# The turned probabilities of an attention kernel: another store queue, other places for weight work, and a last batch that is turned on TensorE

## The reference

```python
qh = (q_in @ wq + bq).reshape(b, q_len, H, K)
kh = (kv_in @ wk + bk).reshape(b, t, H, K)
vh = (kv_in @ wv + bv).reshape(b, t, H, K)
kh = jnp.concatenate([kh, jnp.broadcast_to(bias_k, (b, 1, H, K))], axis=1)
vh = jnp.concatenate([vh, jnp.broadcast_to(bias_v, (b, 1, H, K))], axis=1)
logits = jnp.einsum('bqhk,bthk->bhqt', qh, kh) / scale
weights = jax.nn.softmax(logits, axis=-1)
ctx = jnp.einsum('bhqt,bthk->bqhk', weights, vh).reshape(b, q_len, H * K)
return ctx @ wo + bo
```

## Time and profile before

| | us | share of the span |
|---|---|---|
| median of three runs | 2407.84 | |
| the profiled execution | 2412.1 | |
| its span, 36258 instructions | 2409.9 | |
| PE busy (matmuls) | 2258.8 | 94% |
| PE weight loads (beside the matmuls) | 2027.3 | 84% |
| DVE busy | 1384.3 | 57% |
| ACT busy | 1116.7 | 46% |
| POOL busy | 609.1 | 25% |

### The profile page before, as it was taken

The page is one execution under the profiler, slowest core; times in us unless marked ns, Lnnn a source line. Parts: engine busy times, 40 slices in busy tenths (PEclk is TensorE's granted clock), DMA queues, the critical chain, the costliest instruction groups (busy, mean ns, idle before and its releaser), DMA issues.

```text
span 2409.9 us, 36258 instructions
## 1 busy us (share of the span) xinstructions
PE 2258.8 (94%) x12323; PEld 2027.3 (84%) x12323; DVE 1384.3 (57%) x3102; ACT 1116.7 (46%) x2276; POOL 609.1 (25%) x919
## 2 busy tenths in 40 slices
PE   7999999997999999999988998999998998988999
PEld 6777788897998888898887897988888898977888
DVE  6877863515665665665653525665665565553843
ACT  5777742533444444444433543444444444443421
POOL 2111074401222222222222301222222223122421
PEclk9999999999999999999999999999999999999999
DMA  6322156646877877877864647787887887765110
GB/s 200 120 86 99 62 162 194 211 158 217 276 262 226 274 258 227 273 261 226 277 201 127 211 162 221 255 271 240 259 266 241 263 271 237 236 189 160 57 53 31
DMA packets 326902, 483.18 MB, mean 200 GB/s; under 512 B 65726, under 2 KB 250962, under 8 KB 324674
## 3 DMA queue, kind: packets, MB, share of 16 engines
q1 hardware_dynamic: 326722, 480.87, 61.9%
HBM read 370.30 MB, written 110.49 MB: 200 GB/s over the span
## 4 chain that ended last, share of the span: by engine, by line
PE 67%; DVE 10%; POOL 6%; ACT 6%; issue 6%; DMA 4%; SPq 1%; DVEq 0%; ACTq 0%; POOLq 0%
PE ps_o L1820 7%; PE ps_o L1822 6%; PE ps_o L1821 6%; PE ps_v L1820 5%; PE ps_v L1822 5%; PE ps_v L1821 5%; POOL pt_lo L912 5%; PE ps_k L1820 5%; PE ps_k L1821 4%; PE ps_k L1822 4%; PE ps_s L1820 3%; PE ps_s L1822 3%; PE ps_s L1821 3%; DMA turned_probabilities<-blocks 3%; PE ps_t L1821 2%
## 5 line engine op out<-in xcount | busy, mean ns | idle before, releaser
L1207 ACT ACTIVATE prob<-ps_s,row_columns 128x376 f32<-128x376 f32 x256 | 147.1, 575 | 378.0 <-DVE row_columns L1600 377.9
L912 POOL TENSOR_TENSOR pt_lo<-pt_lo,pt_hi 128x512 fp32r<-128x512 f32 x192 | 245.3, 1307 | 227.2 <-ACT pt_hi L1183 227.2
L904 POOL CAST k_hi<-xk_hi 128x1 fp32r<-128x1 f32 x256 | 52.8, 206 | 895.5 <-PE ps_s L1822 895.5
L1820 PE MATMUL ps_v<-pt_hi,ckd 128*128 128x448 f32 (+1 forms) x384 | 155.1, 404 | 81.4 <-POOL pt_lo L912 63.0
L1820 PE MATMUL ps_k<-cs_hi,w_a_hi 128*128 128x376 f32 x636 | 219.5, 345 | 0.0
L1821 PE MATMUL ps_k<-cs_lo,w_a_hi 128*128 128x376 f32 x636 | 214.7, 338 | 0.0
L1822 PE MATMUL ps_k<-cs_hi,w_a_lo 128*128 128x376 f32 x636 | 213.2, 335 | 0.0
L859 POOL TENSOR_TENSOR w_b_lo<-w_raw_b,w_b_hi 128x512 fp32r<-128x512 f32 x80 | 109.3, 1391 | 349.4 <-ACT w_b_hi L963 349.3
L1616 DVE STREAM_TRANSPOSE blocks<-prob 128x384 f32<-128x384 f32 x256 | 148.1, 579 | 68.4 <-DMA turned_probabilities<-blocks 60.3
L1488 DVE TENSOR_SCALAR prob<-prob,row_columns 128x375 f32<-128x375 f32 (+1 forms) x384 | 177.4, 462 | 4.5
L1485 DVE RECIPROCAL row_columns<-row_columns 128x1 f32<-128x1 f32 (+1 forms) x384 | 62.5, 163 | 196.1 <-ACT prob L1207 188.5
(11 more groups left out here) (290 smaller groups left out, 6391.8 us busy)
## 6 DMA issues: line engine op xcount, KB each, us to landing
ckd<-context_by_key_halves SPq DMA_DIRECT2D x256, 384.0 KB, 5.1
turned_probabilities<-blocks SPq DMA_DIRECT2D x64, 768.0 KB, 3.8
pt_lo<-turned_probabilities SPq DMA_DIRECT2D x256, 192.0 KB, 4.0
cs_hi<-context_halves SPq DMA_DIRECT2D x64, 752.0 KB, 5.8
cs_lo<-context_halves SPq DMA_DIRECT2D x64, 752.0 KB, 7.4
w_raw_b<-in_blocks_b SPq DMA_DIRECT2D x104, 256.0 KB, 3.5
w_raw_a<-in_blocks_a SPq DMA_DIRECT2D x104, 256.0 KB, 4.1
q<-q_scratch SPq DMA_DIRECT2D x64, 256.0 KB, 3.6
```

The source lines that it names most:

```text
L912: pool.tensor_tensor(lo, lo.bitcast(F32), hi, ALU.subtract).then_inc(t_lo, 1)
L1207: act.activation(prob[buf][:, 0:KW], ps_s[buf][:, 0:KW], ACT.Exp, bias=max_neg[:, buf:buf + 1], accum_out=prob_sum[:, buf:buf + 1]).then_i ...
L1820: pe.matmul(out, w_h, m_h, start=first, stop=False)
```

## The change

- **Store.** `store_blocks` goes from SP's queue to ACT's: at t = 2, behind `key_hi` and `sum_hi`, ahead of the exponential. SP keeps the loads.
- **Halves of the turned weights.** `turned_hi` goes ahead of the exponential of t = 0. POOL subtracts by key tile (three instructions of four runs of 128 columns), and `context_sum(0)` waits for one key tile at a time.
- **Weight work.** The split of block b goes from t = 0 and 1 of b2 to t = 2 and 3; the loads go from b2 to b3: block a at t = 0, block b at t = 1 (`fetches`).
- **Queries.** SP's part of the late query pieces goes to the end of its slot.
- **Banks.** Head outputs use ps_o[0] and ps_t[1] in turn and wait for the eviction of the one before the last; the outputs at the end are whole.
- **Last batch of an attend** (`place.final`). Its probabilities aren't stored: PE transposes them (24 transpositions in both attends) into banks, ACT and DVE read halves from there. b6's sum ends in the slots t = 2 and 3; the epilogue has b7's sum, then the head outputs, and rows 0 and 1 of `project` follow them.

Three places show how instructions move; names in these rows are of buffers, and the first word is the line.

The diff, cut to its core:

```diff
+        self.fetches = isinstance(self.b, int) and self.b == 3 and att.layer and group > 0
-        return {0: (0, 1), 1: (2, 3)}.get(t, ()) if self.att.layer and self.loads else ()
+        return {2: (0, 1), 3: (2, 3)}.get(t, ()) if self.att.layer and self.loads else ()
...
+            if place.final and t >= 2:
+                return {2: ((last, 0), (last, 1), (last, 2)), 3: ((last, 3),)}[t]
...
+        def last_bank(t):
+
+            return (ps_t[1], ps_k, ps_t[0], ps_t[1])[t]
...
-            return (ps_o[0], ps_s[0], ps_s[1], ps_t[1])[t] if place.final else ps_o[0]
+            return (ps_o[0], ps_t[1])[t % 2]
...
-                        if query_piece(place, t):
-                            last_query(query, a, skip, query_piece(place, t))
                         if t == 1 and place.after(2):
                             load_q(place.after(2))
                         if t == 2:
                             store_extra(place)
-                            store_blocks(place)
                         if t == 3:
-                            load_turned(place)
+                            if not place.final:
+                                load_turned(place)
                             if place.quarter == 3:
                                 load_extra(place)
                         for head in heads(place, t):
                             store_head(quad_before(place), head)
                         for summed, d in chunks(place, t):
                             load_by_key(summed.next(), d)
-                        if t == 1 and place.loads:
+                        if query_piece(place, t):
+                            last_query(query, a, skip, query_piece(place, t))
+                        if t == 0 and place.fetches:
+                            load_block(0, place.block_a + 1)
+                        if t == 1 and place.fetches:
                             load_block(1, place.block_b + 1)
-                            load_block(0, place.block_a + 1)
...
                 def turned_lo(place):
-                    pool.wait_ge(t_hi, place.visit + 1)
-                    for i in range(3):
-                        part = slice(i * D, (i + 1) * D)
-                        hi, lo = (pt[place.parity][s][:, part] for s in range(2))
+                    pool.wait_ge(t_hi, turned_batches(place) + 1)
+                    for j in range(3):
+                        hi, lo = (key_tile(s, place, j) for s in range(2))
                         pool.tensor_tensor(lo, lo.bitcast(F32), hi, ALU.subtract).then_inc(t_lo, 1)
...
+                def store_blocks(place):
+                    act.wait_ge(block_turn, turned_heads(place, NT))
+                    act.dma_start(turned_scr[place.parity], blocks[:]).then_inc(blocks_out, 16)
+
+                def last_turned_hi(place, t):
+                    act.wait_ge(last_turn, NT * a + t + 1)
+                    if t == 0:
+                        act.wait_ge(c_mm, NT * place.visit - NT)
+                    act.activation(last_place(0, place, t), last_turned(t), ACT.Identity).then_inc(last_hi, 1)
...
-                    wait(act, block_turn, unit_1(place, t) - 1)
+                    if place.final and t >= 2:
+                        act.wait_ge(last_turn, NT * a + t - 1)
+                    elif place.head and place.parity == 0 and t < 2:
+                        wait(act, last_turn, NT * a)
+                    else:
+                        wait(act, block_turn, turned_heads(place, t) - 1)
...
                         for summed, d in chunks(place, t):
                             sum_hi(summed, d)
+                            if place.final and t == 2 and d < 2:
+                                last_turned_hi(place, d + 2)
+                        if t == 0 and place.before():
+                            turned_hi(place.before())
+                        if place.final and t < 2:
+                            last_turned_hi(place, t)
+                        if t == 2 and not place.final:
+                            store_blocks(place)
                         if place.key(t + 2):
                             exp(*place.key(t + 2))
-                        if t == 0 and place.before():
-                            turned_hi(place.before())
...
+                def last_turned_lo(place, t):
+                    dve.wait_ge(last_hi, NT * a + t + 1)
+                    dve.tensor_tensor(last_place(1, place, t), last_turned(t), last_place(0, place, t),
+                                      ALU.subtract).then_inc(last_lo, 1)
...
                 def epilogue(place):
-                    x0 = 5 * RT + 4 * RT * a
-                    dve.wait_ge(early_hi, a + 1)
...
-                    for d in (2, 3):
-                        sum_lo(place.before(), d)
-                    for r in range(EARLY_TILES):
-                        add_y(r, 2 + a, x0, y_bank(1, 0, r))
                     for d in range(DT):
                         sum_lo(place, d)
+                        if d == 1:
+                            dve.wait_ge(early_hi, a + 1)
+                            dve.tensor_tensor(first_outputs_early(early[1]),
+                                              landing(0).rearrange("p (b t r) -> p b t r", t=NT, r=LQ),
+                                              first_outputs_early(early[0]), ALU.subtract).then_inc(early_lo, 1)
+                    for t in range(NT):
+                        output(place, t)
                     for c in range(len(OUT_CHUNKS)):
                         outputs_lo(a, 0, c)
-                    for t in range(NT):
-                        output(place, t)
...
+                def last_turned(place, t):
+                    pe.wait_ge(s_norm, place.unit + t + 1)
+                    if t == 3:
+                        pe.wait_ge(last_lo, NT * a + 1)
+                    for j, (k0, n) in enumerate(KEY_TILES):
+                        last = pe.transpose(last_bank(t)[0:n, j * P:(j + 1) * P], prob[t % 2][:, k0:k0 + n], ident[:])
+                    last.then_inc(last_turn, 1)
...
-                        pe.wait_ge(t_lo, 3 * place.visit + 3)
+                    if d == 0 and place.final:
+                        pe.wait_ge(last_lo, NT * a + NT)
+                        if d == 0 and not place.final:
+                            pe.wait_ge(t_lo, 3 * turned_batches(place) + i + 1)
...
-                def head_output(place, t, part=(0, DT)):
-                    if part[0] == 0:
-                        pe.wait_ge(w_lo[1], 4 * place.block_b + t + 1)
-                        if place.final and t in (1, 2):
-                            pe.wait_ge(s_exp, place.unit + NT)
-                        wait(pe, z_ev, NT * place.quads + (0 if place.final else t))
-                    for c in range(*part):
+                def head_output(place, t):
+                    pe.wait_ge(w_lo[1], 4 * place.block_b + t + 1)
+                    wait(pe, z_ev, NT * place.quads + max(t - 1, 0))
+                    for c in range(DT):
                         if t == 0:
                             pe.wait_ge(c_lo, NT * place.visit + c + 1)
                         last = product(final_bank(place, t)[:, 0:HALF], [w[1][s][:, c, t * P:(t + 1) * P] for s in range(2)],
                                        [heads_view(sums[s][:, c, :], t) for s in range(2)], c == 0, c == DT - 1)
-                    if part[1] == DT:
-                        last.then_inc(z_mm, 1)
-                    elif t == NT - 1:
-                        last.then_inc(z_half, 1)
+                    last.then_inc(z_mm, 1)
...
+                            if place.final and t == 2 and d < 2:
+                                last_turned(place, d + 2)
+                        if place.final and t < 2:
+                            last_turned(place, t)
...
                 def epilogue(place):
-                    for d in (2, 3):
-                        context_sum(place.before(), d)
-                    pe.wait_ge(w_lo[0], 4 * (place.block_a + 1) + 4)
-                    pe.wait_ge(early_lo, a + 1)
-                    for r in range(EARLY_TILES):
-                        project_row(1, 0, 0, 5 * RT + 4 * RT * a, r, early)
                     for d in range(DT):
                         context_sum(place, d)
-                    for part in ((0, 2), (2, DT)):
-                        for t in range(NT):
-                            head_output(place, t, part)
+                    for t in range(NT):
+                        head_output(place, t)
...
+                for r in range(RT):
+                    from_early = group == 0 and r < EARLY_TILES
+                    if from_early:
+                        pe.wait_ge(early_lo, a + 1)
+                    else:
+                        pe.wait_ge(p_lo, 3 * (GROUPS * a + group) + CHUNK_OF[r] + 1)
                     if group == 0 and r == 2:
                         pe.wait_ge(z_ev, NT * QUADS * GROUPS * (a + 1))
```

(33 more changed lines are left out.)

28 lines of the change are left out of this document (10 added, 18 removed).

## The result

The changed kernel takes 2379.11 us in the median of four runs (2377.33 to 2385.06), the kernel before 2409.19 on the same chip; the ratio is 0.9878, 95% interval 0.9857 to 0.9899. It is faster by some 30 us. Forecast were 96, 2312 us, with a range of 2266 to 2362, and 2379 lies outside. The profiled execution took 2377.33, its span is 2375.4 us (2409.9 before).

The account below looks back on a forecast made before the run. PE was taken to bound the kernel, busy 2258.8 of 2409.9 us. Starts -11, plain -10, weight batches -32, b7 +6, ends -15, banks -7, clock -27 sum to -96: 2316.1 as profiled, 2312 us as median, range 2266 to 2362.

Parts of the forecast that it names:

- the plain batches: Batches without weight work: 18 gaps before the first context sum, 12.0 us in all, would shrink by 10.
- weight batches: b2 and b3 of groups 1 to 3: of 44 us of PE's waits 32 would go, 2 staying in each.
- The bound in the text: Weight batches: a gain of only 16 us if the next turned load comes late by 4 to 5 in each.
- The clock: Stretches of PE at half clock: 27 of 37.7 us lost would return, 22 in weight batches, 5 at the ends.
- the starts: Start of both attends: earlier load and waiting by key tile would win 5.6 of a 9.5 us gap, twice: -11.
- the ends: Last batch of both attends: no store or load, PE transposes instead; -15 us, and 5 more from the clock.
- b7's sign: b7, where the next group's queries are split too: PE would wait for DVE instead, a loss of 6 us.
- the wait by key tile: First context sum: waiting for one subtraction at a time would win 1.24 us where POOL ends last.
- the second bank: Head outputs: two banks in turn would hide the wait for evictions, -7 of 8 us.
- Half comes back: Rival, chance 0.22: the store behind `sum_hi` is felt in every batch, some 50 of 96 us given back; 2362.
- the closed ring: Slower rival, chance 0.05: the chain from store to next store, 17.0 us, could reach 20.1 against PE's 17.7; 2461.
- the signs set down beforehand: Profile findings listed as showing the forecast right (fewer than eight half-clock stretches, store about 1.2 after the transposition) or wrong.

Follow-up runs that it names:

- sp_store: The changed kernel with the store back on SP's queue, at t = 2 ahead of the load of context by key; 2343.86 us.
- held_load: The changed kernel, store still on ACT's queue, with SP's load of context by key held back from t = 2 to t = 3; 2333.73 us.
- hi_after_exp: The changed kernel with the rounding of the turned weights behind the exponential of t = 0 again; 2356.00 us.
- after_w5: The changed kernel with the weight loads of b3 put into b5 (t = 0 and 2); 2355.91 us.
- before_weights: The kernel before with the weight work alone moved as in the change, the store on SP; 2387.08 us.
- held_w5: The changed kernel with the load of context by key held back to t = 3 and the weight loads in b5; 2298.53 us.
- after_three: The changed kernel with the first context sum waiting for all three subtractions at once; 2374.44 us.
- after_one_bank: The changed kernel with all head outputs in one bank, each waiting for the eviction of the one before; 2406.09 us.
- the three repairs: The changed kernel with the load of context by key held back, weight loads in b5 and the rounding behind the exponential; 2292.77 us.
- before_act_store: The kernel before with one part alone, the store on ACT's queue at t = 2 behind `sum_hi`; 2454.71 us.

## Why the prediction was wrong

**The step that failed: the plain batches.** It read "the net lies between -0.1 and -1.8 against a gap of 0.67; -10 of 12", with the store 1.1 later and its landing unchanged at 3.8. The store was issued only 0.6 later (median 0.70 after the transposition, 0.09 before: it need not wait for the end of `sum_hi`), but landed 2.0 later. So in the median the data came 2.6 late. With it went the sentence that ACT can start the rounding "when its data is there": it did, but the data was now what it waited for, with the exponential behind: in the median the rounding started 0.02 us after the landing, and 2.28 after it before. 26 plain batches and six b7 cost +35 instead of -4: 39 of the missing 61 us. sp_store and held_load show the landing's part, 35 and 45 us, hi_after_exp the part of the order on ACT, 23; they overlap and aren't to be added.

In the prediction the landing was left at 3.8 with a conclusion from the Trainium skill's "DMA: Bandwidth & Descriptors", section "Issuing engines are not separate DMA queues". What it says, that DMAs from all engines interleave on the same 16, agrees with the traces, and is just what was overlooked: on one queue the store had been served ahead of the load issued after it, and on two they share. 3.3 us without the load and 5.4 with it, in the same batch, are its price. The same section's sentence that issuing on several engines will only save sequencer time doesn't hold for this store: the move cost it 2.0 us of landing. The engine itself made no such difference, since with the load held back the store landed after 4.0 from ACT's queue.

**The second step: weight batches.** "Left I leave 2 us in each" was right for b2 and b3 (-50.4 with the clock, forecast -54), but the bill came one batch later, in b4: +21.2. The bound in the text (-16, if the next turned load comes late by 4 to 5 in each) was near that case, and the sum didn't take it. after_w5 and before_weights show it.

**The clock.** "-27 of 37.7" followed from gaps that would go. As the gaps moved to b4, b7 and plain batches, the stretches at half clock moved with them: 37.0 lost, -0.7. Where the gaps did go, in held_w5, 29 came back.

**Right:** the mechanism at the starts (load and rounding 6.2 and 7.5 earlier), though -17.0 is more than the -11 forecast, with a part of the clock in it that the forecast left there; the ends (-19.8, forecast -20 with the clock), b7's sign (+9.6, forecast +6), the mechanism in b2. **Mis-sized besides:** the wait by key tile, priced at 1.24 where POOL ends last, where after_three finds no gain in the changed kernel; and the second bank, priced at 7, where after_one_bank finds 27. With the three repairs the same change takes 2292.77, 19 under the forecast, so the gains that the forecast lacked were there to be had.

**The rivals.** "Half comes back", 2362, came nearest: it had the store felt in every batch. But its cause, the later issue, was only 0.6 of the 2.6, and what it priced at 50 us over 62 batches came as 35 over 32 and 21 more in six b4, while b6 didn't grow. The slower one, the closed ring, named the right chain, with 17.0 us against PE's 17.7. With 2.0 more for the landing and 0.4 less for the issue it takes some 18.6, 0.9 over PE, and the 26 plain batches grew by 1.0 each; the one shown above took 19.72, as its load back needed 7.0. What would have warned: the margin of 0.7 us between ring and PE was smaller than the spread of the store's landing in the traces of before (3.2 to 6.5).

Of the signs set down beforehand, one for "wrong" came, ACT idle ahead of the rounding with exponentials late behind it; and two for "right" stayed out: there were seventeen stretches at 0.50 instead of fewer than eight, and the store went out 0.70 and not 1.2 after the transposition.

## What to carry to other kernels

In these traces a DMA's place in its queue was a priority (3.8 us to land with the load behind it, 5.8 beside it): before moving a store that a chain of waits hangs on to another engine's queue, look which transfers stood behind it on the old one, since they may then run beside it. Where a path through DRAM closes a ring over a batch, add up the ring and set it against the batch of the engine that bounds; if the margin is less than the spread of landings, as it was here, it can decide. And a burst of loads that is moved out of one batch's way is to be priced in the batch where it arrives, and in the one after.

## What the runs showed of the hardware

Counted in the traces from issue to landing, the same store of 768 KB took

- 3.2 to 3.5 us in the kernel before, in four batches where hardly anything else moved meanwhile (at most 784 KB in all);
- 3.6 to 4.7, median 3.8, in the kernel before, in twenty batches with the load of 384 KB behind it on the same queue and little else;
- 4.5 to 6.0, median 4.7, in before_act_store, in 22 batches with that load issued on the other queue at the same moment and little else;
- 5.5, 5.7 and 7.4 in the changed kernel in three such batches, and 5.9 to 7.8, median 6.0, in eight where the load had been issued 0.45 us ahead of the store;
- 6.7 to 8.4 in the changed kernel beside the weight loads of b3.

In size, 768 + 384 KB in place of 768 is a factor of 1.5, and 1.5 times 3.2 to 3.5 is 4.8 to 5.3. That is near before_act_store and too little for the changed kernel; why the same pair took longer there stays open. The store's own issue takes 0.33 us on ACT's queue, as on SP's.
